# Last layer of a graph network: a fourth of four sender tiles made on chip, message copies on ScalarE, node part in another PSUM bank

## The reference

```python
x = jnp.concatenate([nodes[senders], nodes[receivers], edges], axis=-1)
h = jax.nn.relu(x @ msg_W1 + msg_b1)            # 192 -> 128
messages = jax.nn.relu(h @ msg_W2 + msg_b2)     # 128 -> 64
agg = jax.ops.segment_sum(messages, receivers, num_segments=nodes.shape[0])
y = jnp.concatenate([nodes, agg], axis=-1)
y = jax.nn.relu(y @ node_W1 + node_b1)
y = y @ node_W2 + node_b2
...                                             # layer norm of y, scale, offset
return nodes + y
```

## Time and profile before

| what | value |
|---|---|
| median of 3 runs | 1101.23 us (1100.18 to 1102.29) |
| profiled execution, its own time | 1098.35 us |
| its span, first to last instruction | 1096.6 us |
| span of the last layer's loop (first transposes to those of the last group) | 662.0 to 1073.7 us |
| PE, DVE, ACT, POOL busy over the span | 85%, 75%, 41%, 53% |

### The profile page before, as it was taken

The page is one execution under the profiler, slowest core; times in us unless marked ns, Lnnn a source line. Parts: engine busy times, 40 slices in busy tenths (PEclk is TensorE's granted clock), DMA queues, the critical chain, the costliest instruction groups (busy, mean ns, idle before and its releaser), DMA issues.

```text
span 1096.6 us, 23929 instructions
## 1 busy us (share of the span) xinstructions
PE 928.3 (85%) x6145; PEld 587.6 (54%) x6145; DVE 827.0 (75%) x2605; ACT 449.9 (41%) x887; POOL 586.4 (53%) x763
## 2 busy tenths in 40 slices
PE   2788888799957868677777968999999999999995
PEld 2465565354535656565563664555555555555553
DVE  8988888743578767778885586768777877777876
ACT  2577777211005444444430143444444344344342
POOL 6534333000016777777740037777777777777770
PEclk9687877799988898999888969999999999999998
DMA  3000000700001111111108036545444454454441
GB/s 65 1 1 0 0 0 0 274 19 1 1 14 37 27 26 27 27 26 27 27 16 264 15 83 169 117 109 107 107 102 108 102 102 107 100 106 107 100 98 39
DMA packets 145112, 72.82 MB, mean 66 GB/s; under 512 B 111917, under 2 KB 136698, under 8 KB 144922
## 3 DMA queue, kind: packets, MB, share of 16 engines
q1 hardware_dynamic: 127224, 54.98, 19.0%
q0 software_dynamic: 16448, 16.88, 8.7%
q10 hardware_dynamic: 1378, 0.22, 0.1%
HBM read 59.66 MB, written 12.35 MB: 66 GB/s over the span
## 4 chain that ended last, share of the span: by engine, by line
PE 36%; POOL 26%; DVE 14%; issue 13%; ACT 4%; DMA 3%; DVEq 2%; ACTq 1%; SPq 0%; POOLq 0%
POOL pair L1208 14%; POOL A L1208 12%; PE seg L1606 12%; PE big L1530 4%; PE seg L1733 4%; ACT A L1343 4%; PE big L1769 3%; PE big L1759 2%; DMA A<-table,src_i 2%; PE seg L1780 2%; PE seg L1801 2%; PE seg L1544 2%; DVE acc_mem L2086 1%; PE big L1587 1%; PE seg L1790 1%
## 5 line engine op out<-in xcount | busy, mean ns | idle before, releaser
L1208 POOL DMA_INDIRECT A<-table,src_i x338 | 321.4, 951 | 116.3 <-issue 97.0
L1208 POOL DMA_INDIRECT pair<-table,src_i x176 | 177.0, 1006 | 67.4 <-issue 53.3
L1343 ACT CAST A<-big 128x500 f32 x208 | 125.4, 603 | 48.1 <-PE big L1535 24.9
L1733 PE MATMUL seg<-A 128*128 128x384 f16 (+1 forms) x624 | 120.1, 336 | 10.6 <-DVE A L1960 8.2
L1769 PE MATMUL big<-A 128*128 128x512 f32 x208 | 109.8, 609 | 1.5 <-DMA A<-pr_table 1.5
L1450 ACT ACTIVATE A<-big,A 128x512 f32<-128x512 f32 x104 | 71.5, 688 | 93.3 <-PE big L1770 93.3
L1444 ACT COPY A<-big 128x512 f32<-128x512 f32 x104 | 60.8, 584 | 118.4 <-PE big L1759 118.4
L1733 PEld LDWEIGHTS seg<-A 128*128 128x128 f16 x624 | 57.0, 98 | 89.1 <-issue 35.2
L1636 PE MATMUL big<-A 128*128 128x300 bf16 x480 | 93.9, 343 | 5.4 <-DVE A L1883 4.8
L1397 ACT ACTIVATE pair<-pair,wcol 128x64 f32<-128x64 f32 x176 | 46.8, 336 | 109.9 <-DMA pair<-table,src_i 109.8
L1271 POOL COPY cur<-pair 128x24 bf16 x100 | 39.7, 439 | 95.5 <-PE seg L1544 95.5
(11 more groups left out here) (306 smaller groups left out, 1770.9 us busy)
## 6 DMA issues: line engine op xcount, KB each, us to landing
A<-in_edge_attr_dram SPq DMA_DIRECT2D x103, 128.0 KB
A<-drel_flat SPq DMA_DIRECT2D x104, 126.0 KB
spilled_adjacency<-A SPq DMA_DIRECT2D x1, 7074.0 KB, 21.9
A<-spilled_adjacency SPq DMA_DIRECT2D x6, 1152.0 KB, 11.7
A<-table,src_i POOLq DMA_INDIRECT x338
A<-pr_table SPq DMA_DIRECT2D x104, 31.5 KB
pair<-table,src_i POOLq DMA_INDIRECT x176
A<-low_flat SPq DMA_DIRECT2D x78, 32.0 KB
```

The costliest lines, as they stand in the source:

```text
L1208: pool.indirect_dma_start(out=row, out_offset=None, in_=table, in_offset=bass.IndirectOffsetOnAxis(ap=src_i[:, tile:tile + 1], axis=0)).th ...
L1343: nc.scalar.copy(A[:, :, bass.ds(bases[k], PW)], big[:, k % 4, 0:PC].rearrange("p (s d) -> p s d", d=PW)).then_inc(window_kept, 1)
L1733: op = nc.tensor.matmul(made[:, 0:held.shape[2] * D], hot_low[:, u, m, :], held[:, k, :, :], start=(m == 0 and k == 0), stop=(m == 3 and k ...
```

## The change

`MADE` becomes all of q = 0 to 3, so four tiles of sixteen are made and twelve fetched. SP loads four key rows an iteration. The masks of seven numbers are made for all 104 groups in one instruction ahead of the loop. The copy of the transposed messages moves from VectorE to ScalarE. The nodes' hidden part moves from bank 1 to bank 0 of seg, columns 128 to 255, and stands last in its step on PE; its second product moves from q = 1 to q = 2.

```diff
-MADE = (1, 2, 3)
+MADE = (0, 1, 2, 3)
...
-        chunk_of = carve("l3", NM * (HIGH + 1)).rearrange("p (u s) -> p u s", u=NM)[:, :, 0:HIGH]
+        chunk_of = carve("l3", GROUPS * HIGH).rearrange("p (g s) -> p g s", s=HIGH)
...
+        node_hid = seg[:, 0, P:2 * P]
...
# SyncE, ahead of the loop
-            load_keys(0, G + 2, 0)
+            for u in range(2):
+                load_keys(u, u * G + 2, u)
...
-            keys_ahead(0, Q - 1)
+            for q in range(2, Q):
+                keys_ahead(0, q)
...
# ScalarE
+            def message(it, q):
+                if q % 2 == 0:
+                    return
+                k, h = it * 2 + q // 2, q // 2
+                act.wait_ge(msg_done[1], k + 2)
+                act.wait_ge(seg_done[q], it + (1 + IT1))
+                nc.scalar.copy(msg[:, h, :, :, :].rearrange("p j r d -> p (j r d)"), seg[:, 3, :]).then_inc(msg_ready[1], 1)
...
-            steps(act, [(2, node_relu), (3, copy_rows), (4, hidden), (5, message_relu)])
+            steps(act, [(3, node_relu), (3, copy_rows), (4, hidden), (6, message), (5, message_relu)])
...
# TensorE
-                if nodes_done(it, q, 1):
+                if nodes_done(it, q, 2):
...
-                pe.wait_ge(rows_chosen, it * NM + 1)
-                pe.wait_ge(acc_step, it * Q + (Q + SUMS1 - 2 * Q))
+                pe.wait_ge(acc_step, it * Q + (Q + SUMS1 - 6))
...
-                nc.tensor.matmul(made[:, 0:P], nw1_ah, acc_mem[:, bass.ds(it * P - NODES_LAG * P, P)],
+                nc.tensor.matmul(node_hid, nw1_ah, acc_mem[:, bass.ds(it * P - NODES_LAG * P, P)],
...
+                if q == Q - 1 and not (isinstance(it, int) and not NODES_LAG <= it + 2 < IT):
+                    pe.wait_ge(ev("y1_ready"), it + (3 - NODES_LAG))
...
-            steps(pe, [(0, make_rows), (1, turn_rows), (0, node_hidden), (6, window_sums), (2, hidden_sums), (4, turn_messages), (3, message_sums)])
+            steps(pe, [(0, make_rows), (1, turn_rows), (6, window_sums), (2, hidden_sums), (4, turn_messages), (3, message_sums), (0, node_hidden)])
...
# VectorE
-                dve.tensor_scalar(chunk_of[:, u, :], iota_r[:, 0:HIGH], src_high[:, bass.ds(t, 1)], None, ALU.is_equal).then_inc(ev("chunk_found"), 1)
...
-            def message(it, q):
...
+            link(dve.tensor_tensor(chunk_of, iota_r[:, 0:HIGH].rearrange("p (a s) -> p a s", a=1).broadcast_to([P, GROUPS, HIGH]),
+                                   src_high.rearrange("p (g j) -> p g j", j=G)[:, :, 2:3].broadcast_to([P, GROUPS, HIGH]), ALU.is_equal))
...
-            steps(dve, [(1, receivers), (5, message), (0, senders), (4, plain_hots), (0, node_norm),
+            sender_hots(0, 0)
+            steps(dve, [(1, receivers), (0, senders), (4, plain_hots), (0, node_norm),
```

More of the change, by code:

```diff
@@ L1169, in on_sync @@
                     keys_ahead(IT - 1, q)
+                if q == 2:
+                    load_keys(IT * NM, (IT - 1) * (Q * G) + 2, 0)
                 edge_loads(IT - 1, q, base, G * P if q < Q - 1 else LAST_EDGES)
@@ L1463, in node_relu @@
                 act.wait_ge(ev("y1_ps"), it + (1 - NODES_LAG))
-                nc.scalar.activation(y1_t[:, 0:P], made[:, 0:P], ACT.Relu, bias=nb1_sb).then_inc(ev("y1_ready"), 1)
-            steps(act, [(2, node_relu), (3, copy_rows), (4, hidden), (5, message_relu)])
+                nc.scalar.activation(y1_t[:, 0:P], node_hid, ACT.Relu, bias=nb1_sb).then_inc(ev("y1_ready"), 1)
+            steps(act, [(3, node_relu), (3, copy_rows), (4, hidden), (6, message), (5, message_relu)])
             act.wait_ge(ev("y1_ps"), OUTS[1].start + 1)
@@ L1953, in senders, with sender_hots @@
             def senders(it, q):
-                if (q + 1) % Q not in MADE:
-                    return
-                u = MADE.index((q + 1) % Q)
+                sender_hots(it + (q + 1) // Q, (q + 1) % Q)
+            def sender_hots(it, u):
                 dve.wait_ge(keys_loaded[u], (it + 1) * 16)
@@ L1989, in choose_rows @@
                 m = it * NM + u
-                t = it * (Q * G) + (q * G + 2)
-                dve.tensor_scalar(chunk_of[:, u, :], iota_r[:, 0:HIGH], src_high[:, bass.ds(t, 1)], None, ALU.is_equal).then_inc(ev("chunk_found"), 1)
-                dve.wait_ge(ev("chunk_found"), m + 1)
                 dve.wait_ge(rows_made, m + (NM + 1))
                 dve.tensor_tensor(picked, made.rearrange("p (s f) -> p s f", f=D),
-                                  chunk_of[:, u, :].rearrange("p (s a) -> p s a", a=1).broadcast_to([P, HIGH, D]), ALU.mult).then_inc(ev("picked"), 1)
+                                  chunk_of[:, bass.ds(it * Q + q, 1), :].rearrange("p g s -> p (g s)").rearrange("p (s a) -> p s a", a=1).broadcast_to([P, HIGH, D]), ALU.mult).then_inc(ev("picked"), 1)
                 dve.wait_ge(ev("picked"), m + 1)
@@ L2356 @@
 SHARED = {"ld_edges": "rows_weighed", "sum_ps2": "early_steps", "ow_ready0": "pr_high", "ow_ready1": "pr_middle", "ow_ready2": "keys_loaded0", "ow_ready3": "keys_loaded1",
-          "rstd_in": "senders_ready", "rstd_out": "rows_made", "self_out": "rows_chosen", "self_kept": "chunk_found",
+          "rstd_in": "senders_ready", "rstd_out": "rows_made", "self_out": "rows_chosen",
           "neigh_out": "h_parts_ready", "acc_cleared": "rows2_read", "deg_ps": "chooser_ready", "pads": "sums_cleared",
```

## The result

The changed kernel takes 1128.53 us (median of 4 runs, 1125.5 to 1129.39) against 1101.76 for the kernel before on the same chip: ratio 1.0233, 95% interval 1.0213 to 1.0252. It is 2.3% slower. The forecast was 1128, with a range of 1116 to 1140.

What follows compares the result with a forecast made beforehand. GpSimd's gathers and PE were taken as level, with PE bounding after the change. Front 8.2 + loop 19.7 - drain 0.7 = 27.2 us on 1098.35 gives 1125.6, plus 2.9 for the median: 1128, range 1116 to 1140.

Steps and rivals of the forecast that it cites:

- The bound: Last layer, kernel before: GpSimd's gathers set the pace at about 16.3 us an iteration, PE level with 0.44 us of slack.
- the forecast's PE figure: Last layer's loop, kernel before: without any wait PE would take 15.86 us an iteration, against 16.30 with waits.
- The fourth tile's matmuls, 1.35 us: PE, each iteration: the eight added matmuls cost their distance of starts, 1.35 us, and nothing hides them.
- The first rival: PE has room, as the weight loads' 57% suggests, and GpSimd's 15.1 us sets the pace: some 1075 us; chance 0.04.
- The loop, 17.21: Hardware loop: 15.86 + 1.35 = 17.21 us an iteration without new waits; 21 iterations take 361.4 us, 19.7 more.
- the wait of 0.2: Head of the loop's body: PE waits for VectorE, 8.55 against 8.35 us; taken as 0 more, since 15.86 contains it.
- The third rival: VectorE bounds at step 3, its q = 3 choice delaying the q = 0 matmuls: 1134 to 1142 us; chance 0.17.
- The fourth rival: Cheaper loop: jump back costs nothing and the wait is gone, 16.9 us an iteration, 1121 or 1117 us; chance 0.17.
- ScalarE's copy at nothing: ScalarE, loop: the moved copy of seg's 512 columns, two an iteration, costs PE 0; bounds 0 and 1.2 us.
- The front, 8.2: Ahead of the loop: masks 1.1 us, first steps 4.3 late in all, plus 5.4 for four sets, less 1.5: 8.2 us.
- The drain, -0.7: After the loop: VectorE's copy ahead of the last window additions moves elsewhere, saving 0.7 us.
- The sum: Whole kernel: front 8.2 + loop 19.7 - drain 0.7 = 27.2 us more, giving 1128.

Runs made afterwards that it cites:

- the dropped gather: Kernel before, with the third tile of q = 0 not gathered from the second iteration on, old rows reused, nothing made in its place: 1093.6 us, ratio 0.993.
- the half set: Changed kernel, with the tile of q = 0 made by four of its eight matmuls: 1111.73 us, ratio 1.0085 to the kernel before.
- the first experiment: Kernel before with all edits of the change except the fourth made tile (three made, thirteen gathered): 1101.53 us, ratio 0.9992.
- the norm three steps later: Changed kernel, with VectorE's node norm moved to q = 2 of the next iteration and one more iteration written out ahead: 1124.14 us.
- the last one with late masks: Kernel before with the change minus its fourth tile, masks made during VectorE's wait for the first matmuls, norm placed as in the change: 1102.93 us, ratio 0.9989.
- the norm last: Changed kernel, with VectorE's node norm moved behind the choice of rows: 1132.64 us, ratio 1.0273 to the kernel before.
- the other one with late masks: Kernel before with the change minus its fourth tile, masks made during VectorE's wait for the first matmuls, norm behind the choice of rows: 1104.12 us, ratio 1.0009.
- the control: Changed kernel with six iterations written out ahead of the loop in place of five, nothing else: 1129.39 us, ratio 1.0225 to the kernel before.

## Why the prediction was right, point by point

*The bound.* That PE and GpSimd are level at three tiles holds: the dropped gather gives 15.91 us an iteration, the forecast's PE figure was 15.86.

*The fourth tile's matmuls, 1.35 us.* Shown by the half set: 0.68 for four. The whole exchange, 17.17 - 15.91 = 1.26, agrees: it is 1.35, plus 0.29 of a new wait, less 0.38 that the order before lost and the new one does not (next point). The first rival, room on PE as the weight loads' share suggested, is refuted: that share is 58% in a loop in which PE has nothing left.

*The loop, 17.21.* Measured 17.17, but its make-up was wrong, and that it came so near is in part luck. The prediction worked out that VectorE's chain from the set of q = 2 to the sum of q = 3 takes 8.55 us against PE's 8.35, and then took 0 for the wait of 0.2, since it would fall together with the jump. The arithmetic was good. In the changed kernel the set of q = 2 has this line (PE's timeline):

```profile
906.37 1.52 PE L1746 MATMUL seg<-A 128*128 128x448 f16 x8
```

VectorE's sum ends at 914.94, 8.57 behind it, and PE's next head starts at 915.01, 8.64 behind it. Of these 8.64 PE works 8.35. The step that does not hold is the last one: the jump costs nothing, so there was no loss of the jump for the wait to fall together with. The loop is 16.88 us of PE's own work and 0.29 of waiting for VectorE.

The kernel before must then have had a loss inside its 15.86, which the recorded busy time hides, the ends of matmuls being modelled: 16.88 - 1.35 = 15.53 would be PE alone at three tiles. The kernel with the dropped gather shows it; an iteration there, 891.41 to 907.29, is 15.88. Its head (PE's timeline, then VectorE's):

```profile
906.63 0.60 PE L1790 MATMUL seg<-ident,A 128*128 128x128 f32 x4
907.29 0.65 PE L1759 MATMUL big<-ident,A 128*128 128x128 f32 x4
```

```profile
906.08 0.94 DVE L1998 TENSOR_REDUCE A<-A 128x64 f32<-128x448 f32 x1
```

0.66 where 0.44 is plain, so 0.22 are lost there. It goes with VectorE's sum, which ends at 907.02 while PE is free at 907.07; in the first experiment the sum is early and nothing is lost at the same jump. The earlier trace rows had named VectorE at this place in the kernel before (0.40). Why the transposes start 0.27 behind the sum here, and the matmuls of the changed kernel only 0.07 behind it, is not shown. Two smaller losses make up the rest, when each stage is laid beside that of the kernel with the norm three steps later: 0.06 ahead of the set of q = 3, which starts at 902.86 when the sum that it needs ends at 902.80, and 0.08 around the node part, whose product between the transposes and the hidden sums makes the three take 2.02 us, against 1.94 with the product at the end of the step.

*The third rival* (VectorE as the bound of step 3) was thus half true: its mechanism is there, at 0.29 an iteration of 17.17. It adds nothing to the total, because the 0.29 takes the place of what the 15.86 already held: some 0.33, most of it older waits for VectorE, the larger one at this same spot, where the prediction had put it down to the jump. That old and new losses nearly cancel is chance.

*The fourth rival*, the cheaper loop of 16.9 us, was right that the jump costs nothing and wrong that no wait would be left. With the norm three steps later it is what runs, at 16.885 us.

*ScalarE's copy at nothing.* The first experiment confirms it, and the timeline of the changed kernel has it at the forecast 0.6 us:

```profile
906.71 0.58 ACT L1471 COPY A<-seg 128x512 f32<-128x512 f32 x1
```

It is not waited for in the loop; in the drain it is, by 0.68 us (below).

*The front, 8.2.* Measured 8.7 in the profiled pair, but 1.3 of it lie ahead of the masks. From the instruction shown above (L2276, then L2279) to VectorE's last conversions before the masks, the changed kernel takes 15.26 us and the kernel before 13.95. The kernel before with two made tiles takes 15.25 too, and of the two kernels with late masks one takes 15.26 and the other 13.96. So this is mostly a difference between executions, though all six profiled executions with four made tiles have the longer time, and a share of the change in it is not excluded. That leaves 7.4 us against 8.2. The masks' instruction took 0.92 as estimated and put off the first matmuls by 0.9, where 1.1 was expected. PE's first two sets start at 664.34 and 668.92, a distance of 4.58 where 4.66 was expected. The rest of the difference was not traced.

*The drain, -0.7.* The profiled pair says +0.9, a miss of 1.6 us, but not by this term's own working. The copy's move did help: from the drain's start to the last window sums it is 1112.73 - 1103.78 = 8.95 us, where the earlier trace rows give 9.85. But the matmuls behind them ran at a lower clock, which the prediction had not thought of. The timeline of PE after:

```profile
1112.73 1.12 PE L1815 MATMUL seg<-A 128*128 128x84 f32 x8 [0.68 <-ACT A L1471]
1114.79 2.04 PE L1825 MATMUL seg<-acc_mem,A 128*128 128x512 f32 x2 [0.93 <-DVE acc_mem L1888]
1117.60 1.97 PE L1828 MATMUL big<-A 128*128 128x64 f32 x8 [0.78 <-ACT A L1482]
```

and of before:

```profile
1085.55 1.12 PE L1811 MATMUL seg<-acc_mem,A 128*128 128x512 f32 x2 [0.93 <-DVE acc_mem L1874]
1087.45 1.10 PE L1814 MATMUL big<-A 128*128 128x64 f32 x8 [0.78 <-ACT A L1469]
```

2.04 + 1.97 against 1.12 + 1.10 is 1.8 us more, and the last section shows that this comes and goes without the change.

*The sum.* With what differs between executions taken out (2.76, 1.3 and 1.8 us), the profiled pair is some 25 us apart: 7.4 in front, 18.6 in the loop, -0.9 in the drain. The forecast had 27.2. The medians are 26.8 apart. So the forecast is right to about 2 us, and that it lies within 1 us of the measured median is more than its working can claim.

## What to carry to other kernels

When two engines are level, moving work from one to the other gains at most the slack of the receiver and costs the whole of what it receives: read both per iteration, from distances of starts, before looking at the price of the piece. Here the trade was 0.40 us for 1.35. And when a chain through a second engine comes out longer than the bounding engine's own steps, even by 0.2 us, count it: do not let a jump or another loss that nobody has measured absorb it.

Place small dependent work by where its engine waits, not by where its input is ready: the same five VectorE instructions cost 0.29, 0.44 or 0 us an iteration in three places.

## What the runs showed of the hardware

The jump back of the hardware loop cost TensorE nothing: 0.44 us from the transposes to the next set across the jump, the same as inside the body.

A run of indirect gathers goes at one per 1.25 us with 0.94 recorded, and the 0.30 pause holds also when everybody waits for the gathers (14 in 17.7 us). Where GpSimd is not the bound, single gathers are recorded longer: one an iteration at some 1.37 us in the changed kernel, two at 1.3 to 1.47 with the thirteenth gather kept, none with the norm three steps later (0.94 us on average).

The granted clock fell in the drain. The windows view of the changed kernel, 1104 to 1113 and 1113 to 1120 us, clock in the third column from the right:

```profile
1104.00:1113.00 9.00, 7.94 (x44) 4.35 (x43) 4.80 (x22) 4.78 (x8) 0.00 (x0) 1.00 0.01 3
1113.00:1120.00 7.00, 4.86 (x18) 2.95 (x17) 3.81 (x5) 0.69 (x1) 0.00 (x0) 0.63 0.18 39
```

From 1.00 to 0.63, a mixture of the two levels of 2.4 and 1.2 GHz; before the fall PE had been busy through the loop and then waited in short pieces in the drain. It does not belong to the change. In the kernel before, the clock fell as well, but later, behind these matmuls (0.57 from 1090 to 1100 us). The first group of matmuls behind the last window sums (L1811 before, L1825 after), 1.12 us there and 2.04 here, took 2.0 to 2.1 us in the kernels with half the matmuls, with the kept and with the dropped gather, with the norm three steps later and in the last one with late masks; 1.12 or 1.13 in the first experiment, with the norm last and in the other one with late masks; and 1.34 and 1.37 in the control and with two made tiles. The second group (L1814, L1828) took 1.58 to 1.97 in all of these. What decides it was not tried; it is worth up to 1.8 us to whoever compares two profiled executions.
